# Local projections one iteration earlier in a two-layer attention and mixture-of-experts kernel, with its stores, shift rows and row sends rearranged

## The reference

```python
# layer 0: sliding-window attention (16 heads of 8), then layer norm
allowed = (j <= i) & (j >= i - 128)
attn = softmax(where(allowed, q @ k.T * 8**-0.5, -inf))
x = layernorm(x + (attn @ v) @ w_out.T)
# layer 1: pre-norm causal attention, then a mixture of 8 experts, top 2
h = layer_norm(x); x_resid = x + causal_attention(h) @ w_o
xf = layer_norm(x_resid)
top_w, top_i = top_k(softmax(xf @ w_gate), 2); top_w /= top_w.sum()
out = sum over e of gate_e * (gelu(xf @ w1[e] + b1[e]) @ w2[e] + b2[e])
x = layernorm(x + out + x_resid)
```

## Time and profile before

| what | us |
|---|---|
| median of 3 runs | 868.08 |
| lowest and highest | 866.9 and 868.32 |
| the profiled execution, its own time | 870.4 |
| the profiled execution, span | 868.6 |
| PE busy | 655.7 |
| DVE busy | 509.7 |
| ACT busy | 462.6 |
| POOL busy | 429.8 |

### The profile page before, as it was taken

The page is one execution under the profiler, slowest core; times in us unless marked ns, Lnnn a source line. Parts: engine busy times, 40 slices in busy tenths (PEclk is TensorE's granted clock), DMA queues, the critical chain, the costliest instruction groups (busy, mean ns, idle before and its releaser), DMA issues.

```text
span 868.6 us, 19900 instructions
## 1 busy us (share of the span) xinstructions
PE 655.7 (75%) x7512; PEld 393.1 (45%) x7512; DVE 509.7 (59%) x1116; ACT 462.6 (53%) x671; POOL 429.8 (49%) x649
## 2 busy tenths in 40 slices
PE   2557978978887878888788888886614999999900
PEld 0323434434443433444343444442313998898900
DVE  1644667676776888798888879882340222222236
ACT  2035655655674565766677666666502554554503
POOL 4015556556654543245464647458640454445445
PEclk8568999998997998999999999999855999999965
DMA  5635544643643637334362707101014566566464
GB/s 170 157 90 115 138 109 100 154 126 67 159 116 46 153 97 135 102 76 135 66 159 42 185 25 190 43 16 53 20 58 161 187 204 214 184 223 213 168 163 128
DMA packets 73583, 107.45 MB, mean 124 GB/s; under 512 B 8104, under 2 KB 60048, under 8 KB 70428
## 3 DMA queue, kind: packets, MB, share of 16 engines
q1 hardware_dynamic: 68892, 97.86, 42.2%
q0 software_dynamic: 4608, 8.47, 3.3%
HBM read 44.14 MB, written 38.90 MB: 96 GB/s over the span
## 4 chain that ended last, share of the span: by engine, by line
PE 32%; DMA 22%; DVE 17%; issue 10%; SPq 7%; POOL 6%; ACT 4%; another core or an unknown queue 0%; POOLq 0%; ACTq 0%; DVEq 0%
DMA parts_dram<-parts 9%; DMA arena<-parts_dram 7%; PE pair_ps L1415 6%; PE o_ps L1278 6%; SPq L439 4%; PE o_ps L1434 3%; PE pair_ps L1299 3%; PE pair_ps L1198 3%; POOL rows_dram L628 3%; DMA rows_dram<-rows,row_at 3%; PE misc L1434 3%; DVE row_max L878 2%; ACT probs L707 2%; DVE row_max L876 2%; PE pair_ps L1258 1%
## 5 line engine op out<-in xcount | busy, mean ns | idle before, releaser
L707 ACT ACTIVATE probs<-pair_ps 128x1024 f32<-128x1024 f32 x272 | 275.4, 1022 | 116.2 <-PE pair_ps L1198 107.5
L1278 PE MATMUL o_ps<-probs,v_aug 128*32 128x256 f32 (+3 forms) x2048 | 166.0, 421 | 9.1 <-POOL probs L616 3.5
L603 POOL TENSOR_SCALAR_AFFINE_SELECT probs<-probs 128x512 f32<-128x512 f32 x96 | 61.2, 637 | 140.4 <-ACT probs L707 139.4
L1198 PE MATMUL pair_ps<-arena 50*128 50x256 bf16 (+3 forms) x1024 | 108.2, 288 | 26.6 <-DMA arena<-shift_t 6.5
L673 POOL DMA_INDIRECT outputs_dram<-o_norm,arena x80 | 77.7, 971 | 100.5 <-DVE o_norm L1128 80.0
L867 DVE TENSOR_REDUCE row_max<-pair_ps 128x4 f32<-128x768 f32 x96 | 89.7, 953 | 46.7 <-PE pair_ps L1232 46.1
L838 ACT ACTIVATE probs<-pair_ps,arena 128x256 f32<-128x256 f32 x160 | 65.4, 471 | 76.3 <-PE pair_ps L1415 66.0
L876 DVE TENSOR_REDUCE row_max<-pair_ps 128x2 f32<-128x1024 f32 x64 | 77.2, 1219 | 15.8 <-PE pair_ps L1258 14.7
L1415 PE MATMUL pair_ps<-x_t,arena 128*128 128x256 f32 x320 | 80.8, 397 | 7.1 <-DMA arena<-pack 3.9
L1198 PEld LDWEIGHTS pair_ps<-arena 50*128 50x128 bf16 x1024 | 32.7, 95 | 108.9 <-issue 45.5
L1278 PEld LDWEIGHTS o_ps<-probs,v_aug 128*32 128x32 f32 x2048 | 48.6, 111 | 66.0 <-issue 39.5
(11 more groups left out here) (147 smaller groups left out, 1107.8 us busy)
## 6 DMA issues: line engine op xcount, KB each, us to landing
arena<-pack SPq DMA_DIRECT2D x40, 578.0 KB
arena<-parts_dram SPq DMA_DIRECT2D x96, 192.0 KB
parts_dram<-parts SPq DMA_DIRECT2D x32, 384.0 KB
parts_dram<-parts SPq DMA_DIRECT2D x32, 256.0 KB
arena<-rows_dram SPq DMA_DIRECT2D x40, 130.0 KB
pack<-in_pack SPq DMA_DIRECT2D x8, 578.0 KB, 7.4
parts_dram<-parts SPq DMA_DIRECT2D x32, 128.0 KB
arena<-parts_dram SPq DMA_DIRECT2D x32, 128.0 KB
```

The source lines that it names most:

```text
L707: nc.scalar.activation(probs[:, n % PROBS, :], pair_ps[RING_AT["score", n][0]][:, :, :].rearrange("p b t -> p (b t)"), ACT.Exp, scale=SCAL ...
L1198: last = nc.tensor.matmul(pair[:, r, col:col + width], k_st[u % STACKS][own, gs, j * P:(j + 1) * P], q_st[u % STACKS][own, gs, q0:q0 + wid ...
L1278: last = nc.tensor.matmul(o_ps[c * VHEAD:(c + 1) * VHEAD, q0:q0 + width], v_aug[u % 2][:, j, first:first + VHEAD], probs[:, slot, r * T + ...
```

## The change

- A local unit `it+3` (units 2 to 7) is projected at step 8 of iteration `it`, instead of step 0 of iteration `it+1`. Causal units stay at step 1 of iteration `it`.
- The scratch is doubled (`u % 2`), so a store waits for the loads of unit `u-2`. Units from 2 on store all three parts and then load 48 rows in each of four DMAs, instead of ten DMAs of 24, 16 and 8 rows. Units 0 and 1 keep the ten loads. A local unit's stores are issued at the end of SP's part of the iteration, its loads at the head of the next.
- No maxima of unit 1 stand in iteration -1; its 14 maxima share the 11 steps of iteration 0.
- The two sends of the shift rows are issued by ACT, which waits for its own copy first, instead of SP.
- `rows` and `row_at` exist twice. The eight indirect DMAs of a unit stand behind the masks of steps 1, 3, ... 15.
- Moments, variances and `apply` come one step earlier, POOL's root before the mask of step 10. `xf` moves from step 14 to 13, the row copy from 16 to 13, `rank` from 18 to 19, with `place` at step 0 of the next iteration; `top_two` is first in its step.

The core of the diff:

```diff
-        if u - 2 >= -1:
+        if u - 2 >= 0:
...
-    CAUSAL: {0: ("xt",), 2: ("v",), 5: ("on",), 7: ("out",), 14: ("xf",), 15: ("shift",), 16: ("logits",), 18: ("rank",)},
+    CAUSAL: {0: ("xt",), 2: ("v",), 5: ("on",), 7: ("out",), 13: ("xf",), 15: ("shift",), 16: ("logits",), 19: ("rank",)},
...
-    if it < 0:
-        return k if it == -2 and 0 <= k < 2 else None
-    return it + 2 if real(it + 2) and k == (0 if layer(it + 2) == LOCAL else 1) else None
+    if it == -2:
+        return k if 0 <= k < 2 else None
+    if k == 8 and real(it + 3) and layer(it + 3) == LOCAL:
+        return it + 3
+    return it + 2 if k == 1 and real(it + 2) and layer(it + 2) == CAUSAL else None
...
+            def store_parts(u):
+
+                if u >= 2:
+                    sp.wait_ge(stack_in[(u - 2) % STACKS], stacks_in(u - 2))
+                store(u, HIGH, high_ready)
+                store(u, MIDDLE, middle_ready)
+                store(u, LOW, low_ready)
+
             def load_stacks(u):
...
-                if u:
-                    sp.wait_ge(stack_in[(u - 1) % STACKS], ((u - 1) // STACKS + 1) * STACK_LOADS)
-                store(0, high_ready)
-                store(1, middle_ready)
                 if u >= STACKS:
                     sp.wait_ge(score_filled, BEFORE[u - STACKS + 1])
-                sp.wait_ge(stored_high, (u + 1) * 32)
+                for part in (HIGH, MIDDLE, LOW):
+                    sp.wait_ge(stored[part], (u + 1) * 32)
                 for side in range(2):
-                    load(side, *HIGH_ROWS[side])
-                store(2, low_ready)
-                sp.wait_ge(stored_low, (u + 1) * 64)
+                    load(u, side, 0, STACK_K)
...
-                if real(it + 1):
-                    load_shift(it + 1)
+                if it >= -1 and real(it + 3) and layer(it + 3) == LOCAL:
+                    store_parts(it + 3)
...
                 for k in range(steps(it)):
+                    if real(w) and k == 10:
+                        root(w)
                     if real(it):
                         mask(it, k)
-                    if real(w) and k == 10:
-                        root(w)
...
-                    if real(it - 2) and layer(it - 2) == CAUSAL and k < CHOICES:
-                        send(it - 2 - B, k)
+                    if real(it - 2) and layer(it - 2) == CAUSAL and k % 2 and k < 2 * CHOICES:
+                        send(it - 2 - B, k // 2)
...
                 nc.scalar.activation(shift_t[:, :], misc[0:4 * GS, :], ACT.Copy).then_inc(misc_taken, 1)
+                act.wait_ge(misc_taken, JOB["shift", u])
+                for r in range(TILES_R):
+                    nc.scalar.dma_start(q_st[u % STACKS][HALF * r + STACK_K:HALF * r + SCORE_K, :, :],
+                                        shift_t[2 * GS * r:2 * GS * (r + 1), :]).then_inc(shift_in[u % STACKS], 16)
...
                     if real(w):
+                        if k == 8:
+                            moments(w)
                         if k == 9:
-                            moments(w)
-                        if k == 10:
                             variances(w)
-                        if k == 12:
+                        if k == 11:
                             apply(w)
```

136 lines of the change are left out of this document (77 added, 59 removed).

## The result

The changed kernel takes 876.44 us in the median of seven runs (872.13 to 885.46), the kernel before 868.08 beside it (863.39 to 870.18). The ratio is 1.010, with a 95% interval of 1.007 to 1.013: one per cent slower, where 853.5 us was forecast. The profiled execution took 876.77 us, its span is 875.0.

What follows compares the result with a forecast made beforehand. It took PE's stops for the stack, about 16 us in local iterations 0 to 5, as what the long DMA chain costs. Terms +4, 0, -9.8, -4.2, -2.8, +2.8, 0, -3, -1.7 sum to -14.7: 868.1 to 853.5 us, range 844 to 865.

Steps and rivals of the forecast that it cites:

- Stops for the stack: PE's waits for stacks ahead of local maxima, 43.1 us in eight: gone in iterations 0 to 5 except the start's first.
- rival B: Local iterations 0 to 4: DVE's shift work makes the maxima's split 2.5 us late, PE stops there instead; 863.5 us, chance 0.17.
- The start, +4 taken: Up to the first scores: waiting for unit 2's `x_t` and projecting it there costs about 4 us net, between -3 and +7.
- transpose, copy, send and landing 4.2, as now: Last step of the start's sum: first shift's transpose to landing takes 4.2 us as before, first scores at about 62.
- Local iterations, -14 taken: Local iterations 1 to 5, stops for the stack gone: -9.8 us for iterations 1 to 4 and -4.2 for iteration 5.
- 28.6 each: Length of local iterations 1 to 4: iteration 2 at full clock less its stop, 28.0 us, and 0.6 charged; 114.4 in all.
- the charge of 0.6 us: Local iterations: two shift subtractions on DVE ahead of the maxima's split, charged at 0.6 us an iteration instead of 2.45.
- ACT's sends, +2.8 taken: Shift rows sent by ACT: nothing in local iterations, 0.4 us in each of seven causal ones; bounds 0 and 21.
- Rival C: Every unit: ACT's two issues and its wait stand in full, 1.4 us 15 times, 21 us; slower, 871.6 us, chance 0.12.
- Iteration 15, -3 taken: Iteration 15: eight sends spread over 16 steps shorten its first half by 3 us, between -1 and -5.
- Iteration 16, -1.7 taken: Iteration 16: DVE's 2.24 us wait for the sends shrinks, POOL's root then being the limit; -1.7 us, bounds 0 and -2.2.
- The second `rows` buys 0.: Causal iterations: a second copy of `rows` gains 0, as iterations 9 (no sends) and 10 (eight sends) were equal.

Runs made afterwards that it cites:

- E2: Changed kernel with the shift rows' sends given back to SP, behind its stores and ahead of the stack loads; 865.29 us, ratio 0.998 to the kernel before.
- E15: E5 run again, on the chip of E13 and E14: changed kernel, local projection back at step 0, SP's sends; median 836.7 us, ratio 0.976.
- E14: E3 run again, on the chip of E15: changed kernel with unit 2's `x_t` loaded early and SP's sends, projection still early; ratio 0.987.
- E17: Kernel before with whole loads alone: units from 2 on store all three parts, then load 48 rows in each of four DMAs; ratio 0.994.
- E5: Changed kernel with the local projection back at step 0 and the shift rows' sends back on SP, all else kept; 839.3 us, ratio 0.977.
- E13: Changed kernel with only the local projection back at step 0, ACT keeping the shift rows' sends; median 847.5 us, ratio 0.989.
- E4: Kernel before with the shift rows' sends moved to ACT and nothing else; 882.92 us, ratio 1.023.
- E8: Kernel before with the second `rows` and row numbers and the spread sends alone; ratio 1.001.
- E16: Kernel before with the moved steps alone (moments, variances, `apply`, root, `xf`, row copy, `rank` with `place`, `top_two`); ratio 0.999.
- E18: Kernel before with the moved steps and whole loads together, nothing else; ratio 0.997.
- E3: Changed kernel with two edits: unit 2's `x_t` loaded behind unit 1's low store, and SP sending the shift rows; 857.56 us, ratio 0.990.

## Why the prediction was wrong

Forecast and measured by stretch, the measured from the marks of the two profiled executions (us, after less before, rounded):

| stretch | forecast | measured |
|---|---|---|
| start and iteration 0, to shift 1 | +4 | +12.4 |
| iterations 1 to 5, to shift 6 | -14.0 | -3.4 |
| iterations 6 and 7, to shift 8 | -2.8 | -4.2 |
| to shift 15 | +2.8 | +0.5 |
| to the last output transposes | -3 | +2.4 |
| from there to the end | -1.7 | -1.4 |
| sum | -14.7 | +6.4 |

The spans are 875.0 and 868.6. The forecast for ACT's sends stands in one row; what they cost is spread over several. The -1.4 of the last stretch is within what it differs by between profiles of one chip.

**Stops for the stack, right.** All local ones went (18.3 us is left, the start's), and rival B's place was named: PE now waits for DVE's shift, 10.8 us in eight, 4.56 of it once at the start. Ahead of causal maxima the waits fell from 4.9 us to one of 1.8; the stretches of iterations 6 and 7 are 2.5 and 1.7 us shorter, 4.2 where 2.8 was taken:

```profile
PE pair_ps L1287 <- DMA arena<-parts_dram: 1.8, 1, 1.8
```

By the Trainium skill, "DMA: Bandwidth & Descriptors", section "Why a DMA increments its semaphore by 16 and not by 1", a copy of 48 rows uses more of the 16 engines than one of 24 or 8. I had worked out from it that the wait would go whole, -4.9; the size of the gain lies nearer to that than my term did, and 1.8 us are left. No run here shows the split itself.

**The start, +4 taken.** `x_t` came at 47.36, as forecast (about 47), and PE stood 8.34 us for it. The step that failed is the next: "transpose, copy, send and landing 4.2, as now", so first scores at about 62. They came at 70.24. I had followed the send to ACT and the loads of unit 2 within SP's queue, but hadn't asked what is on its way when the send leaves. E2 has its first scores at 61.99 with the sends ahead of the loads, and so shows the cause. The effect of this stop on the end is small: it is made up by shift 7.

**Local iterations, -14 taken, -3.4 measured.** Two steps failed. The first is "28.6 each", which gives every iteration the full granted clock once the stop is gone: three of the five, 31.3, 31.8 and 30.6 us long, still have a granted clock of 0.84 to 0.89. The second is the charge of 0.6 us for the two subtractions on DVE. The base of 28.0 can be had: E15, with the projection at step 0 and SP's sends, has two local iterations of 27.8 us at full clock, beside one of 30.8. With the early projection the shortest at full clock take 28.9 (E14, SP's sends) and 29.3 (the kernel after). And the comparison was the wrong one: the stops go with the loads made whole (E17, and E5 without the early projection), so the early projection must pay for itself and doesn't. It costs 1.1% (E14 against E15), 6.5 us of it at the start.

**ACT's sends, +2.8 taken.** The step that failed is that in the causal iterations ACT "can catch up". It can't: 1.41 us stand in front of the exponential (1.4 was the price put on one), and 10 to 11 us in all reach the end, 1.2% (E2 against after) and 1.3% (E15 against E13). On the kernel before it is 2.3%, or 14.3 us between the medians (E4). Nor were the sends free in the local iterations, where they were priced at nothing: from shift 0 to shift 7 E13 takes 220.9 us and E15 215.6, E4 225.2 and the kernel before 220.2. Rival C had the right mechanism and place. Its 21 us were the bound; half of it came here, two thirds in E4.

**Iteration 15, -3 taken.** After it is 2.4 us longer behind shift 15, not shorter. From 592 to 604 PE runs at a granted clock of 0.65:

```profile
592.00:604.00 12.00, 10.37 (x75) 3.84 (x77) 2.39 (x14) 6.91 (x9) 6.53 (x14) 0.65 0.04 12
```

E2, without ACT's sends, needs 36.3 us there against 39.7 before. In the same stretch, 590 to 604, its granted clock is 1.00. E15, with SP's sends, needs 36.2 us, and E13, with ACT's, 38.4. So the gain exists, -3.4, and ACT's sends took it; it isn't shown that the spread sends made it, since E8, with these alone, needs 39.1.

**Iteration 16, -1.7 taken.** The wait for the sends is gone and one of 1.16 us for POOL's root stands in its place, as named:

```profile
639.35 2.91 DVE L1007 TENSOR_SCALAR rows<-y,mean_var,rstd 128x128 f32<-128x128 f32 x4 [1.16 <-POOL rstd L666]
```

But the four operations now take 2.91 us instead of the 1.62 of the earlier trace rows, and that eats it.

**"The second `rows` buys 0."** Right for the kernel before (E8), wrong with the moved steps (E16 and E18 against E15), on which the causal layer then rests. That iterations 9 and 10 were equal before said nothing on it: DVE came to its rows a step later then, and waited for the sends 4.4 us in all. The steps that move it and the rows that free it had to be priced together.

In per cent of the time, the way from after to E15 is 1.2 for the sends (E2), 0.8 for `x_t` (E3 behind E2) and 1.1 for the projection (E14 to E15). That is 3.1 of 3.4; the rest is the 0.35 by which E3 differs between two chips. From before to E15, 2.4 in all, whole loads alone have 0.6. The rest is shared by second rows with moved steps, the first maxima's place and the second scratch; how it splits among them is open, except that none of them, put on the kernel before or taken out of E5 by itself, moved the ratio by more than half a per cent. Why local iterations still fall to a lower granted clock, three of five in the kernel after and two of them in E15 (0.95 and 0.89), is open too.

## What to carry to other kernels

A DMA issue costs the engine that issues it: 1.4 us for two small sends and the wait ahead of them, on an engine that is idle a third of the time, came through to the end by some two thirds of a microsecond in each of 16 units, because the engine's next instruction was the one the others wait for. Before a transfer is moved to another engine, list what is in flight when it leaves; 1.5 MB ahead of 32 KB made 10 us. And test the costly edit by taking it out of the finished change, not only by adding it to the old kernel: the edit that the sum relied on was a loss, while two edits that were worth nothing alone, the second rows with the spread sends and the moved steps, were worth 1.5 us an iteration or more together.

## What was not expected of the hardware

- The small sends had a queue of their own and still landed 10.4 us after their issue began, behind four loads of 384 KB; in E2 SP's, issued 1.4 us ahead of such loads, were in after 2.9 us.
- Four operations of DVE on 128x128 f32 took 2.49 us with POOL's masks running beside them and 1.11 without, in one kernel (E15).
- A send issued by ACT takes as long as one by SP did, 621 ns against 619 in the median; the longest took 1259, at the start, against 682:

```profile
L816 ACTq DMA_DIRECT2D arena<-shift_t x32: 620/621/1259, 59.9 to 589.8; - x32
```

- The same stage, from the last output transposes to the end, took 234.0 to 248.5 us in different profiles, and it goes by the chip: 234.0 to 238.2 on two chips and 242.7 to 248.5 on the others. Two kernels that differ only ahead of it are better compared by where it begins.
